# GNN and FFN kernel: edge tables made in the first stage, hidden rows stored by SyncE, combination with full-row products

## The reference

```python
edge_index = jnp.stack([src, dst])
x = x + _L0_gnn_ref(_layernorm(x), edge_attr_4, edge_attr_8, edge_index, ...)
x = x + _L0_ffn_ref(_layernorm(x)[None], ...)[0]
x = x + _L1_gnn_ref(_layernorm(x), edge_index, ...)
x = x + _L1_ffn_ref(_layernorm(x)[None], ...)[0]
```

```python
x0, x1 = _lin_irreps(x0, x1, W_up0, W_up1)              # node rows
h = edge_feats                                          # 8 attributes
for W in (W_mlp1, W_mlp2, W_mlp3):
    h = SILU_2MOM * silu(h @ W / sqrt(W.shape[0]))      # 64 hidden
tpw = h @ W_mlp4 / sqrt(64)                             # 4 x 128 path weights
...                                                     # messages of 4 attributes, sender row, tpw
msg0 = segment_sum(m0, receiver)
```

```python
gw = _topk_gate(x @ wg_group, 2, 4)
z = _layernorm(x, ln_g, ln_b)
for g in range(4):
    iw = _topk_gate(z @ wg_inner[g], 2, 8)
    moe = sum_e iw[:, e] * (relu(z @ W1[g, e] + b1) @ W2[g, e] + b2[g, e])
    out = out + gw[:, g] * _layernorm(z + moe, gln_g[g], gln_b[g])
return out + inp
```

## Time and profile before

| | us |
|---|---|
| median of 3 runs | 2750.76 (2745.88 to 2754.09) |
| profiled execution | 2753.15 |
| its span in the trace | 2751.4 |
| `prepare`, from the span's start | to about 121.8 |
| `edges` | 121.9 to 890.0 |
| `update`, gates and experts | 890.0 to 1400.4 |
| combination | 1400.4 to 1543.2 |

### The profile page before, as it was taken

The page is one execution under the profiler, slowest core; times in us unless marked ns, Lnnn a source line. Parts: engine busy times, 40 slices in busy tenths (PEclk is TensorE's granted clock), DMA queues, the critical chain, the costliest instruction groups (busy, mean ns, idle before and its releaser), DMA issues. The chain is left out here.

```text
span 2751.4 us, 37847 instructions
## 1 busy us (share of the span) xinstructions
PE 2077.5 (76%) x11841; PEld 1302.3 (47%) x11842; DVE 1521.5 (55%) x2398; ACT 1210.0 (44%) x1768; POOL 788.2 (29%) x747
## 2 busy tenths in 40 slices
PE   5557777777776544999977368899999999436777
PEld 2224344334343544777732143777345775234454
DVE  2048888888887156333345368777584773163111
ACT  5557778887775211455520021666004661011111
POOL 1286666666664000344452000000000000002232
PEclk8868888888888755899965569999999999757898
DMA  3434444444443430577542311300002101254672
GB/s 123 149 94 129 130 130 128 129 129 130 127 131 89 133 126 10 196 271 270 192 135 75 103 49 39 102 19 1 16 37 68 37 1 53 74 196 114 174 204 53
DMA packets 202894, 300.26 MB, mean 109 GB/s; under 512 B 114567, under 2 KB 121426, under 8 KB 198710
## 3 DMA queue, kind: packets, MB, share of 16 engines
q0 software_dynamic: 100896, 152.33, 19.7%
q1 hardware_dynamic: 101910, 146.80, 17.0%
HBM read 243.71 MB, written 54.95 MB: 109 GB/s over the span
## 5 line engine op out<-in xcount | busy, mean ns | idle before, releaser
L485 POOL DMA_INDIRECT p_s<-node_table,p_srci x320 | 462.2, 1444 | 145.9 <-issue 74.2
L526 ACT ACTIVATE p_of<-p_node_ids,p_rise 125x1252 bf16<-125x1252 f16 x320 | 426.6, 1333 | 10.0 <-PE p_psC L685 6.5
L1903 PE MATMUL g_psO<-g_h,g_ring 125*125 125x257 f32 x1600 | 373.0, 388 | 20.3 <-DVE g_ring L2035 11.0
L667 PE MATMUL p_psW<-p_w,p_hid 64*125 64x512 f32 x640 | 203.8, 669 | 205.1 <-ACT p_w L521 175.0
L1903 PEld LDWEIGHTS g_psO<-g_h,g_ring 125*125 125x125 f32 x1600 | 297.1, 190 | 92.8 <-DVE g_stage L2029 26.5
L675 PE MATMUL p_psM<-p_msg,p_to 125*32 125x384 f32 x648 | 303.6, 627 | 27.1 <-DVE p_msg L597 20.7
L597 DVE TENSOR_TENSOR p_msg<-p_w,p_s 125x1536 f32<-125x1536 f32 x160 | 273.6, 1751 | 0.0
L521 ACT ACTIVATE p_w<-p_psW 125x512 f32<-125x512 f32 x320 | 188.9, 590 | 162.7 <-PE p_psW L667 162.3
L679 PE MATMUL p_psM<-p_msg,p_to 125*32 125x256 f32 x648 | 257.9, 488 | 0.0
L678 PE MATMUL p_psM<-p_msg,p_to 125*32 125x256 f32 x648 | 248.5, 473 | 0.0
L677 PE MATMUL p_psM<-p_msg,p_to 125*32 125x256 f32 x648 | 240.4, 511 | 0.0
(11 more groups left out here) (336 smaller groups left out, 3852.4 us busy)
## 6 DMA issues: line engine op xcount, KB each, us to landing
p_ring<-in_L_ffn_weights SPq DMA_DIRECT2D x32, 1025.0 KB
slot_rows<-p_y POOLq DMA_DIRECT2D x70, 256.0 KB, 4.3
p_w1s<-in_L_ffn_w SPq DMA_DIRECT2D x16, 1024.0 KB, 9.3
p_w2s<-in_L_ffn_w SPq DMA_DIRECT2D x16, 1024.0 KB
hidden<-p_h POOLq DMA_DIRECT2D x40, 250.0 KB, 3.8
p_hid<-hidden SPq DMA_DIRECT2D x160, 62.5 KB
g_rb<-receiver_rows SPq DMA_DIRECT2D x16, 610.4 KB
p_x<-x SPq DMA_DIRECT2D x3, 2500.0 KB
```

The costliest lines, as they stand in the source:

```text
L485: pool.indirect_dma_start(s[:, b, c, :, :].rearrange("p k u -> p (k u)"), None, node_table, bass.IndirectOffsetOnAxis(ap=srci[:, b, c:c + ...
L526: nc.scalar.activation(of[:, b, c, :], node_ids[:], ACT.Sigmoid, scale=STEEP, bias=rise[:, bass.ds(g, 1), c:c + 1].rearrange("p o c -> p ( ...
L667: nc.tensor.matmul(psW[c % 2][0:P, :], hid[part, b, c // 2, :], w4[part, :], start=True, stop=True)\
L1903: last = nc.tensor.matmul(psO[0:P, j, 0:HW], ring[:, i % RING, j * P:(j + 1) * P], h[:, s, hd, :], start=s == 0, stop=s == T - 1)
```

## The change

Three parts.

1. The tables of the edge loop become an object of their own (`EdgeTables`), which lives through `prepare` and `edges`. SyncE loads the lists, attributes and `w4` in `prepare` behind x, `dst` and `wu`, and `table` and `base` after iteration LEAD + 2; GpSimd makes the constants and clears `macc` and `cacc` as its first work; VectorE's `prepare_once` stands at the end of its stream in `prepare`, while the memsets of PSUM stay in `edges`; ScalarE scales `w4` at iteration LEAD + 3. `edges` has no waits for tables any more. `ea` has four buffers of iterations (EB = 4), and four iterations are loaded ahead of x.
2. The hidden rows, `steps` and `bases` are stored by SyncE's queue. GpSimd stores node rows alone.
3. In the combination all of TensorE's products have 128 rows: `small` and `wide_t` are padded with zeros by GpSimd. gln_b's product is one (its gates, the undecided ones of the groups, stand in four more columns of `wide`), and the products of tile t are in three functions: sums (waits for out_ok of t - 2), gains (wait for `scaled`, VectorE's first two operations of `finish` of t - 1), and offsets two tiles ahead.

```diff
@@ prepare
+    EB = 4
...
-        ea = sb("ea", [128, 2, EG])
+        ea = sb("ea", [128, EB, EG])
...
-                    if i >= 2:
-                        sp.wait_ge(mm1, (i - 1) * B)
+                    if i >= EB:
+                        sp.wait_ge(mm1, (i - EB + 1) * B)
                     for b in range(B):
-                        sp.dma_start(ea[32 * b:32 * b + 16, i % 2, :], ea8[i * B + b]).then_inc(ea_in[i % 2], 16)
+                        sp.dma_start(ea[32 * b:32 * b + 16, i % EB, :], ea8[i * B + b]).then_inc(ea_in[i % EB], 16)
...
-                load(0)
-                load(1)
+                for i in range(EB):
+                    load(i)
                 rows = x.rearrange("(t p) d -> p t d", p=P)
                 for k in range(T // 2):
                     sp.dma_start(xs[:, 2 * k:2 * k + 2, :], rows[:, 2 * k:2 * k + 2, :]).then_inc(x_in[k], 16)
+                sp.dma_start(dsts[:], dst.rearrange("(g e) -> g e", e=EG)).then_inc(dst_in, 16)
                 sp.dma_start(wu[:, 0, :], w_up0).then_inc(up_in, 16)
                 sp.dma_start(wu[:, 1, :], w_up1).then_inc(up_in, 16)
-                sp.dma_start(dsts[:], dst.rearrange("(g e) -> g e", e=EG)).then_inc(dst_in, 16)
-                for i in range(2, ITER):
-                    load(i)
+                sp.dma_start(tables.dst_rows[:].rearrange("p g c -> p (g c)"), dst_p).then_inc(all_in, 16)
+                sp.dma_start(tables.src_rows[:].rearrange("p g c -> p (g c)"), src).then_inc(all_in, 16)
+                sp.dma_start(tables.y[:].rearrange("p g c m -> p (g c m)"), ea4).then_inc(all_in, 16)
+                for half in range(2):
+                    sp.dma_start(tables.w4[half * HID:(half + 1) * HID, :], w_mlp4).then_inc(all_in, 16)
+
+                for i in range(ITER):
+                    if i + EB < ITER:
+                        load(i + EB)
+                    for b in range(B):
+                        sp.wait_ge(h3_ok, i * B + b + 1)
+                        sp.dma_start(hidden[(i * B + b) * 128:(i * B + b) * 128 + 128, :], h3[:, b, :])\
+                            .then_inc(h3_out[b], 16)
+                    if i == LEAD + 1:
+                        sp.wait_ge(tab_ok, 1)
+                        sp.dma_start(steps, tabi[:]).then_inc(tab_out, 16)
+                        sp.dma_start(bases.rearrange("(g o) -> g o", o=1), ext[:, 0:1]).then_inc(tab_out, 16)
+                    if i == LEAD + 2:
+                        sp.wait_ge(tab_out, 32)
+                        sp.dma_start(tables.table[:], steps.unsqueeze(0)).then_inc(table_in, 16)
+                        sp.dma_start(tables.base[:], bases.partition_broadcast(128)).then_inc(table_in, 16)
+                for b in range(B):
+                    sp.wait_ge(h3_out[b], 16 * ITER)
...
-                for i in range(ITER):
-                    for t in tiles_after(i):
-                        pool.wait_ge(us_ok, t + 1)
-                        pool.dma_start(node_table[t * P:(t + 1) * P, :], us[:, t % 2, :]).then_inc(us_out[t % 2], 16)
-                    for b in range(B):
-                        pool.wait_ge(h3_ok, i * B + b + 1)
-                        pool.dma_start(hidden[(i * B + b) * 128:(i * B + b) * 128 + 128, :], h3[:, b, :])\
-                            .then_inc(h3_out[b], 16)
-                pool.wait_ge(tab_ok, 1)
-                pool.dma_start(steps, tabi[:]).then_inc(tab_out, 16)
-                pool.dma_start(bases.rearrange("(g o) -> g o", o=1), ext[:, 0:1]).then_inc(tab_out, 16)
+                nc.gpsimd.iota(tables.columns[:], [[1, WIN]], base=0, channel_multiplier=0,
+                               allow_small_or_imprecise_dtypes=True).then_inc(ids, 1)
+                nc.gpsimd.iota(tables.row_id[:], [[0, 1]], base=0, channel_multiplier=1).then_inc(ids, 1)
+                nc.gpsimd.iota(tables.node_ids[:], [[1, NW]], base=-1, channel_multiplier=0,
+                               allow_small_or_imprecise_dtypes=True).then_inc(ids, 1)
+                nc.gpsimd.iota(tables.blocks[:], [[1, WINS]], base=0, channel_multiplier=0,
+                               allow_small_or_imprecise_dtypes=True).then_inc(ids, 1)
+                nc.gpsimd.memset(tables.macc[:], 0.0).then_inc(ids, 1)
+                nc.gpsimd.memset(tables.cacc[:], 0.0).then_inc(ids, 1)
+                pool.wait_ge(ids, 6)
+
+                for t in range(T):
+                    pool.wait_ge(us_ok, t + 1)
+                    pool.dma_start(node_table[t * P:(t + 1) * P, :], us[:, t % 2, :]).then_inc(us_out[t % 2], 16)
...
-                pool.wait_ge(tab_out, 32)
-                for b in range(B):
-                    pool.wait_ge(h3_out[b], 16 * ITER)
...
+                base, row_id, dst_rows, masked = tables.base, tables.row_id, tables.dst_rows, tables.masked
+                block_of, column = tables.block_of, tables.column
+                v.wait_ge(all_in, 16 * 5)
+                v.wait_ge(ids, 6)
+                tick(nc.vector.tensor_scalar(tables.rise[:], tables.src_rows[:], -STEEP, 0.5 * STEEP, ALU.mult, ALU.add))
+                n_row = tick(nc.vector.tensor_scalar(row_id[:], row_id[:], WIN - 1, None, ALU.bitwise_and))
+                tick.wait(n_row)
+                n_row = tick(nc.vector.tensor_copy(rowf[:], row_id[:]))
+                v.wait_ge(table_in, 32)
+                n_rel = tick(nc.vector.tensor_tensor(scratch[:], dst_rows[:],
+                                                     base[0:P, :].unsqueeze(2).broadcast_to([P, G, C]), ALU.subtract))
...
+                tick(nc.vector.tensor_tensor(block_of[:], block_of[:],
+                                             window_of[:].unsqueeze(2).broadcast_to([P, G, C]), ALU.add))
+                tick.wait()
...
-                    pe.wait_ge(ea_in[i % 2], 64 * (i // 2) + 64)
+                    pe.wait_ge(ea_in[i % EB], 64 * (i // EB) + 64)
...
+                    if i == LEAD + 3:
+                        act.wait_ge(all_in, 16 * 5)
+                        nc.scalar.activation(tables.w4[:], tables.w4[:], ACT.Copy, scale=SILU_GAIN / 8.0)
@@ edges
-                sp.dma_start(table[:], steps.unsqueeze(0)).then_inc(table_in, 16)
-                sp.dma_start(base[:], bases.partition_broadcast(128)).then_inc(table_in, 16)
-                for half in range(2):
-                    sp.dma_start(w4[half * HID:(half + 1) * HID, :], w_mlp4).then_inc(w_in, 16)
-                sp.dma_start(dst_rows[:].rearrange("p g c -> p (g c)"), dst).then_inc(all_in, 16)
-                sp.dma_start(src_rows[:].rearrange("p g c -> p (g c)"), src).then_inc(all_in, 16)
-                sp.dma_start(y[:].rearrange("p g c m -> p (g c m)"), ea4).then_inc(all_in, 16)
...
-                pool.wait_ge(all_in, 48)
...
-                        if first and b:
-                            nc.gpsimd.memset(macc[:], 0.0).then_inc(zeroed, 1)
-                            nc.gpsimd.memset(cacc[:], 0.0).then_inc(zeroed, 1)
...
-                act.wait_ge(w_in, 32)
-                nc.scalar.activation(w4[:], w4[:], ACT.Copy, scale=SILU_GAIN / 8.0).then_inc(w4_ok, 1)
...
-                act.wait_ge(table_in, 32)
-                act.wait_ge(consts, 4)
-                act.wait_ge(rise_ok, 1)
...
-                def prepare_once():
-                    tick = Ticks(v, once)
-                    v.wait_ge(consts, 4)
-                    v.wait_ge(table_in, 32)
-                    v.wait_ge(all_in, 48)
-                    for i in range(3):
-                        tick(nc.vector.memset(psM[i][:], 0.0))
-                    nc.vector.tensor_scalar(rise[:], src_rows[:], -STEEP, 0.5 * STEEP, ALU.mult, ALU.add).then_inc(rise_ok, 1)
...
-                prepare_once()
+                cleared = Ticks(v, once)
+                for i in range(3):
+                    cleared(nc.vector.memset(psM[i][:], 0.0))
+                cleared.wait()
...
-                v.wait_ge(zeroed, 2)
...
-                pe.wait_ge(table_in, 32)
-                pe.wait_ge(w4_ok, 1)
@@ routed_experts
-    M = X + NG
+    M = X + 2 * NG
+    ROWS = 128
...
-        small = sb("small", [M, 3, D])
+        small = sb("small", [ROWS, 3, D])
...
+                    sp.wait_ge(zeros, 1)
                     sp.dma_start(small[0:X, 0, :], b2.rearrange("g e d -> (g e) d")).then_inc(small_in, 16)
-                    sp.dma_start(small[X:M, 1, :], gln_g).then_inc(small_in, 16)
-                    sp.dma_start(small[X:M, 2, :], gln_b).then_inc(small_in, 16)
+                    sp.dma_start(small[X:X + NG, 1, :], gln_g).then_inc(small_in, 16)
+                    sp.dma_start(small[X + NG:M, 2, :], gln_b).then_inc(small_in, 16)
...
+                    nc.gpsimd.memset(small[:], 0.0).then_inc(zeros, 1)
+                    pool.wait_ge(zeros, 1)
...
-                        tick(nc.vector.tensor_tensor(wide[:, :, a, X:M], gate[:, :, 0, 0:NG], group, ALU.mult))
```

(53 more changed lines are left out.)

144 lines of the change are left out of this document (68 added, 76 removed).

## The result

The changed kernel takes 2666.84 us (median of 4 runs, 2666.09 to 2668.64), the kernel before 2750.61 beside it: a ratio of 0.9698, 95% interval 0.9681 to 0.9714. Forecast were 2670 and a range from 2656 to 2700. The profiled execution took 2668.64 us, its span is 2666.9, so the two spans differ by 84.5 us.

| stage, us | before | after | change | forecast |
|---|---|---|---|---|
| network, up to SyncE's first issue of the edge loop | 121.84 | 122.45 | +0.6 | +1.8 |
| edge loop, up to the first store of counts | 770.44 | 738.62 | -31.8 | -33.8 |
| counts, update, gates and experts | 508.13 | 510.25 | +2.1 | +0.3 |
| combination | 142.77 | 94.64 | -48.1 | -49.0 |
| all behind it, code not touched | 1208.2 | 1200.9 | -7.3 | 0 |

What follows compares the result with a forecast made beforehand. Bound by engines waiting for each other at the edge loop's start and in the combination. 2753.15 - 33.8 + 1.8 - 49.0 + 0.3 = 2672.5 profiled; runs' median lies 2.4 lower, so 2670 us, range 2656 to 2700.

Steps and rivals of the forecast that it cites:

- Both places: Edge loop start: VectorE waits 21.74 us while GpSimd clears cacc; combination: VectorE waits 5.29 us per period for TensorE's L1518.
- Part 1: Edge loop: with tables loaded and buffers cleared ahead, 33.8 us off, bounds 31 to 36.
- The step to the third group: Edge loop: third group's gathers issued 17.1 us after stage start, its messages starting at 30.0 us.
- kept behind, where the loop is untouched: Edge loop after the third group: the 33.8 us gained at its start stay gained to the end.
- the memsets and the table work cost nothing: Network: both fit idle time of GpSimd and VectorE; uncovered they would cost 24.1 and up to 7.2 us.
- Part 2: Network: hidden rows stored by SyncE delay iteration 2 by 6.2 us; edge loop starts 1.2 us later, 1.8 with w4.
- the end of the stage: Network end: last hidden store lands in 3.8 us at 118.2, `bases` before at 117.0; next stage 4.8 us after landing.
- Scaling w4: Network: scaling w4 on ScalarE, which sets the pace there, costs 0.6 us.
- Part 3: Combination: padded products raise the clock, TensorE's chain goes, VectorE becomes the bound at 7.33 us a tile: -49.0 us.
- The low clock: Combination: the clock stays low despite padding, TensorE is the bound, -25.7 us instead of -49.0, so 2693 us; chance 0.12.
- Hidden stores at 128 GB/s: Network: hidden stores held to 128 GB/s on SyncE's queue, edge loop +14 us instead of +1.2, so 2683 us; chance 0.10.
- The late buffer: Network, ScalarE's wait for h3_out: hidden buffer returns so late that the kernel is slower, 2760 us; chance 0.03.

Runs made afterwards that it cites:

- the kernel that clears late: The changed kernel, waits clamped at zero in the further-windows branch, with macc and cacc cleared behind the second group's gathers as before: 2709.87 us, ratio 0.9814.
- the control: The changed kernel with only the waited values in the branch for further windows clamped at zero: 2684.74 us, ratio 0.9712.
- the combination alone: The kernel before with `routed_experts` as changed, waits clamped at zero in the further-windows branch: 2704.09 us, ratio 0.9815.
- the two controls: The changed kernel with waits clamped at zero in the further-windows branch, run on two chips: 2684.74 and 2666.3 us, ratios 0.9712 and 0.9693.

## Why the prediction was right, and where it was not

**What bounds it.** Both places were read rightly. The wait of 21.74 us for cacc and the one of 5.29 us for L1518 are gone, and nothing took their place in their stages.

**Part 1.** The step to the third group holds: 29.7 us into the stage, forecast 30.0, shown from its other side by the kernel that clears late. One thing on the way is luck: the first group's messages start at 134.87, 12.4 us into the stage as forecast, but what releases them is ScalarE's path weights (9.38 us, L567) and not the gathers. The loop as a whole lost 31.8 and not 33.8 us: the third group is 34.1 us earlier within the stage than before, but the end of the loop only 31.8. The old loop took 770.4 and 772.0 us in two traces and the new one 737.9 to 739.6 in five, which leaves 31 to 34 us, so it isn't shown that "kept behind, where the loop is untouched" failed. That the memsets and the table work cost nothing in the network holds: nothing waits for either there, and the kernel that clears late has a network of 122.8 us, not a shorter one.

**Part 2.** +0.6 against +1.8 looks right, but two terms were off by about 5 us each. The first: I had iteration 2 start at 45.7, it was 47.99, and I had all that follows 6.2 us later, it was 11.7. The first hidden store was issued at 37.79, forecast 36, and released ScalarE at 47.26, forecast 45: 2.3 us. What stands ahead of it was forecast well: VectorE starts on x's pieces at 20.07, 24.08, 28.07, 32.68 and 36.86, forecast 20, 24, 28, 32 and 36. The other 3.2 are longer iterations behind it, 9.6 us for iteration 2 (before 8.6) and 13.4 for iteration 4 (before 11.4). Iteration 4 is a matter of the clock; before, then after:

```profile
54.45:65.80 11.35, 9.57 (x68) 5.18 (x66) 6.61 (x18) 11.00 (x20) 2.44 (x5) 1.00 0.40 126
```

```profile
64.10:77.50 13.40, 11.96 (x68) 6.49 (x66) 6.61 (x18) 11.35 (x20) 0.80 (x1) 0.75 0.32 98
```

The same 68 products take 11.96 us at a grant of 0.75, 9.57 at 1.00. It would be easy to blame the 24 us for which TensorE stood before, but the grant was back at 1.00 from 58 to 66, and two other traces speak against it: first the control, where TensorE stands as long (its iteration 2 starts at 48.22), then the combination alone, which has the old network:

```profile
64.23:75.61 11.38, 9.61 (x68) 5.20 (x66) 6.61 (x18) 11.02 (x20) 0.80 (x1) 1.00 0.40 116
```

```profile
54.91:68.37 13.46, 12.02 (x68) 6.56 (x66) 6.60 (x18) 11.35 (x20) 2.44 (x5) 0.75 0.34 106
```

So this low stretch comes and goes between traces of the same code, and it is worth 2 us: the new network takes 120.4 to 121.2 us in the three traces without it and 122.4 to 122.8 in the three with it (121.7 in the seventh, at a grant of 0.86), the old one 121.8 without and 124.4 with. Like compared with like, the network became 0.6 to 2.0 us shorter, where +1.8 was forecast. The second: the end of the stage. I priced it with 3.8 us to land and 4.8 to the next stage, the latter read at GpSimd's queue; on SyncE's queue it is 2.99 us from the last issue to the next stage, and 3.1 and 3.3 in the two kernels with x on GpSimd's. The kernel with hidden rows on GpSimd has 7.47 there, so this goes with the queue. Scaling w4 was priced at 0.6 us and cost nothing: the iteration with it starts at 94.80 and the next at 103.43, 8.63 us as before. ScalarE waits some 0.4 us for TensorE in such an iteration, and the scaling went into that wait. That the queue behind x holds the first hidden stores is shown by three kernels: iteration 2 starts at 34.4 with the stores elsewhere, at 28.4 with x elsewhere behind ea, at 48.0 as changed. Moving the stores to that queue did not pay by itself: undone, the ratio is 0.9697 (0.967 to 0.972), and 0.9712 (0.968 to 0.975) for the control beside it.

**Part 3.** -48.1 against -49.0; the period is 7.22 us against 7.33, and VectorE is the bound. What did not hold is the reason that was given. I held the clock to decide which engine is the bound, and with it the padding. For padded products at the low clock that sum may hold; no run had it. But without padding TensorE nearly keeps pace at the low clock, 7.57 us a tile, because gains and offsets run side by side. The padding is worth 2.3 us on top of the order (96.97 to 94.64), not 23; the seven other traces with the changed combination have 92.6 to 95.4 us, so it is 2 to 4, and the ratios don't tell the two kernels apart. A slip in the working is small: with the 6.1 us a tile that it states, the second and third tile are there at 1420.1 and 1426.2 and not at 1419.2 and 1425.8, up to 0.9 us. The number came out since VectorE's pace is what is left by either way.

**The other terms.** Counts, update, gates and experts took 2.1 us more, 0.3 was forecast. The two kernels with the old `routed_experts` have 508.1 and 508.6 in this stretch, the nine others 509.0 to 513.2 and the changed one 510.3; that the change costs some 1 to 2 us here fits, its cause was not sought. The 7.3 us behind the combination are not the change's: in ten traces beside it the stretch takes 1197.2 to 1208.2 us, the two controls lie at 1208.2 and 1198.5. The forecast of 0 was right. In the profiled pair these 7.3 us are luck: without them its difference would be 77 us, where 81 was forecast.

**The rivals.** The low clock: grant 0.84 over the combination, it fell. Hidden stores at 128 GB/s: iterations of 8.63 us and 3.4 us to land (median), it fell; its own sum, 45.3 + 39 x 2.0 + 24 x 0.25, is 129.3 and not 131.3. The late buffer: its place was right, ScalarE stood 24.30 us at `h3_out`, but once and not in each iteration.

## What to carry to other kernels

Where TensorE and VectorE wait for each other in a chain, price breaking the chain and raising the clock apart before doing both: here the order gave 45.8 of 48.1 us at the low clock, and the padding 42.7 in the old order. Before pricing small products one by one, look whether they run side by side. Stores that free a buffer don't belong on a queue behind bulk loads, and bulk loads of another queue can still hold up small ones, here ea until 20.2 us instead of 9.5: x had to be moved and to be issued after ea, which gave another 11.4 us. And a difference in a stage whose code is the same is first measured on the same kernel twice, and on which chip is noted with it: here it was 7 us, and in the edge loop once 24.

## What the runs showed of the hardware

TensorE busy all of the time with products on 8, 32 and 125 rows kept a grant of 0.50 for 70 us, while products on 128 and 125 rows that kept it busy 66 to 82% of two such stretches had 1.00. Products on rows 0 to 31 and 32 to 39 ran side by side, two passes in 0.85 us at the low clock. From the last issue on GpSimd's queue to the next stage it took 7.47 us in one trace, on SyncE's 2.99 to 3.3 in three. Loads of x on 125 partitions had a DMA share of 0.33 at 128 GB/s on SyncE's queue, and on GpSimd's, with a few small loads beside them, 1.03 at 212 GB/s. With x issued first on GpSimd's queue the first ea of SyncE's queue landed at 20.23 us and not at 9.5. Hidden rows of 250 KB landed up to 2.6 us apart beside loads on another queue. The same 68 products of an iteration took 9.6 us in two traces and 12.0 in two others, with a grant of 1.00 and 0.75, and which it was did not go with the code.
